# Attention in a graph network on one core: the softmax's reciprocal as exp(-ln S) on ScalarE with a Newton step on VectorE, and half of its products one step later

## The chip, the core and the metric

The kernel runs on one core of a Trainium2 chip, as one launch. A core has TensorE (PE: matmuls, PEld: their weight loads), VectorE (DVE), ScalarE (ACT), GpSimd (POOL) and SyncE (SP), each with its own queue that is worked off in order; they meet only at semaphores. The metric is the device time of one execution in microseconds (us).

## The reference

Four graph layers run one after the other on 512 nodes with 512 features, each as `x = x + layer(relu(layernorm(x)))`. The first layer holds what is changed here. Its softmax runs over the heads (`axis=1` of `n h m`), not over the nodes:

```
q = (x @ Wq + bq).reshape(N, H, HEAD)      # N = 512, H = 8, HEAD = 64
k = (x @ Wk + bk).reshape(N, H, HEAD)
v = (x @ Wv + bv).reshape(N, H, HEAD)
scores = jnp.einsum('nhd,mhd->nhm', q, k) / np.sqrt(HEAD)
scores = jnp.where(adj[:, None, :] == 0, -1000000000.0, scores)
attn = jax.nn.softmax(scores, axis=1)
attn_out = jnp.einsum('nhm,mhd->nhd', attn, v).reshape(N, D_OUT)
h1 = _layer_norm(x + attn_out @ Wo + bo, g1, be1)
ff = jax.nn.relu(h1 @ W1 + b1) @ W2 + b2
return _layer_norm(h1 + ff, g2, be2)
```

After it come a mean over edges with two products, four experts of two layers with a gate, and a last layer with normalised degrees.

## The kernel before

Everything stays in the core's memory. Float32 matrices are split into a high and a low part, and a product of two takes three matmuls. The weights, 27 matrices of 1 MB, come in through two staging buffers; ScalarE makes the high part and GpSimd the low part. In the first 95 us the kernel also counts the edges into a 512 x 512 matrix.

Attention is worked off in STEPS = 8 steps. Step i handles 128 of the m nodes (`i % 4`) against 256 of the n nodes (`i // 4`), for all 8 heads: a tile of 128 partitions x 8 heads x 256 columns. The heads go in two groups of four, g = 0 and 1. For each step:

- TensorE, `scores(i, g)` (L1212, L1216): masks with `no_edge` and multiplies k by q into the accumulator banks.
- ScalarE, `coarse_scores(i, g)` (L573): copies a group's scores to bf16.
- VectorE, `maxima(i)` (L814, L816, L819): the maximum over the heads, `m_bf`.
- TensorE, `centre(i, g)` (L1223): subtracts the maximum from the scores.
- ScalarE, `exponentials(i)` (L559): two Exp, one for each group, 128 x 1024 each, into one of three buffers `e_sb`.
- VectorE: the sum S over the heads in three additions (L836 to L838), its reciprocal (L839), and `probabilities` twice (L352), which multiplies four heads at a time by 1/S.
- TensorE, `values(i, part_no)` (L1238): multiplies the probabilities by v, two steps later, a group at a time.

Each queue is written out by hand, in this order. VectorE's loop body i begins with `maxima(i + 1)`, then sums, reciprocal and products of step i; body 5 has `attended_lo(0)` (L824) in between. ScalarE's body i is `exponentials(i)`, `coarse_scores(i + 1, 1)`, in body 5 `attended_hi(0)`, then `coarse_scores(i + 2, 0)`. TensorE's body i is `centre(i, 0)`, `centre(i, 1)`, `values(i - 2, 0)`, `scores(i + 1, 1)`, `values(i - 2, 1)`, `scores(i + 2, 0)`. Behind the last step VectorE goes on with the first layer norm (`h1_start(0)`, L850). Activation functions of the kernel before are Copy, Identity, Relu, Abs and Exp; it never asks for Ln.

Of the kernel before, what the change touches and what calls it, by code (L numbers as in the profile page):

```python
# [26 lines left out]
ACT = mybir.ActivationFunctionType  # L27
F32 = mybir.dt.float32
# [6 lines left out]
P = 128  # L35
# [4 lines left out]
def build(nc, d, out):  # L40
# [6 lines left out]
    HEADS = 8  # L47
# [4 lines left out]
    HN = N // 2  # L52
    STEPS = 2 * NT
# [14 lines left out]
    def region(size):  # L68
        start = at[0]
        at[0] += size  # L70
        return start

    def place(name, shape, dt, offset):
        return nc.alloc_sbuf_tensor_at(name, shape, dt, offset=offset)

    MAT = NT * D * 4
    rW, rX, rH, rT, rCT, rQK, rVZ, rEP, rM = (region(k * MAT) for k in (6, 1, 1, 2, 2, 4, 4, 3, 1))
# [13 lines left out]
    k_sb = place("k_sb", [P, PAIRS, N], F32, rQK + MAT)  # L91
    v_sb = place("v_sb", [P, NT, D], F32, rQK + 2 * MAT)
    half_sum = place("half_sum", [P, HEADS // 2, HN], F32, rQK + 3 * MAT)
    ff_hi = place("ff_hi", [P, FT, N], F32R, rQK)
    ff_lo = place("ff_lo", [P, FT, N], F32R, rQK + 2 * MAT)
    R_hi = place("R_hi", [P, NT, D], F32R, rQK)
# [40 lines left out]
    rsum = place("rsum", [P, 2, HN], F32, rS)  # L137
# [94 lines left out]
    with ctx:  # L232
        ps = ctx.enter_context(nc.psum_tensor("ps", [P, 8, 512], F32))

        def sem(name):
            return ctx.enter_context(nc.semaphore(name))
# [26 lines left out]
        rinv_made = sem("rinv_made")  # L263
# [16 lines left out]
        coarse_made, max_read = sem("coarse_made"), sem("max_read")  # L280
        score_done, max_done, centred = sem("score_done"), sem("max_done"), sem("centred")
        exp_done, prob_done = sem("exp_done"), sem("prob_done")
        pv_done = sem("pv_done")
        att_hi_made, att_lo_made = sem("att_hi_made"), sem("att_lo_made")
        bo_added, b2_added, be2_added, bias1_added = sem("bo_added"), sem("b2_added"), sem("be2_added"), sem("bias1_added")
# [51 lines left out]
        def group_scores(i, g):  # L337
            bank = slot_bank(i, g)
            return ps[:, bank:bank + 2, :].rearrange("p b (w n) -> p w b n", w=2)
# [5 lines left out]
        def attended():  # L345

            return ps[:, 0:2, :].rearrange("p b (w n) -> p (b w) n", w=2)

        def probabilities(engine, i, heads):

            e = e_bufs[i % E_BUFS][:, heads]
            return engine.tensor_tensor(e, e, rsum[:, i % 2:i % 2 + 1, :].to_broadcast(list(e.shape)), ALU.mult)  # L352
# [61 lines left out]
        def _(gp):  # L414
# [31 lines left out]
            def add_row(i, t, target, done):  # L446
                slot = rows_in[i][1]
                if t == 0:
                    gp.wait_ge(row_in[slot], 16 * (1 + sum(s == slot for _, s in rows_in[:i])))
                ins = gp.tensor_tensor(target[:, t, :], target[:, t, :], row[slot][:], ALU.add)  # L450
                ins.then_inc(done, 1)
# [37 lines left out]
        def _(act):  # L489
# [63 lines left out]
            def exponentials(i):  # L553
                for g in range(2):
                    if i >= E_BUFS:
                        act.wait_ge(pv_done, 2 * (i - E_BUFS) + g + 1)
                    act.wait_ge(centred, 2 * i + g + 1)
                    heads = e_bufs[i % E_BUFS][:, g * HEADS // 2:(g + 1) * HEADS // 2]
                    nc.scalar.activation(heads.rearrange("p (w b) n -> p w b n", w=2), group_scores(i, g), ACT.Exp,  # L559
                                         scale=SCALE).then_inc(exp_done, 1)  # L560

            def attended_hi(half):
                act.wait_ge(pv_done, 2 * NT * (half + 1))
                nc.scalar.activation(T_hi[:, :, half * HN:(half + 1) * HN], attended(), ACT.Copy)\
                  .then_inc(att_hi_made, 1)

            def coarse_scores(i, g):

                act.wait_ge(score_done, 2 * i + g + 1)
                if i >= 1:  # L570
                    act.wait_ge(max_read, i)
                heads = s_bf[:, g * HEADS // 2:(g + 1) * HEADS // 2]
                nc.scalar.activation(heads.rearrange("p (w b) n -> p w b n", w=2), group_scores(i, g), ACT.Copy)\  # L573
                  .then_inc(coarse_made, 1)
# [3 lines left out]
            coarse_scores(1, 0)  # L578
            for i in range(STEPS):
                exponentials(i)  # L580
                if i + 1 < STEPS:
                    coarse_scores(i + 1, 1)
                if i == NT + 1:
                    attended_hi(0)
                if i + 2 < STEPS:
                    coarse_scores(i + 2, 0)
            attended_hi(1)
            for t in range(NT // 2):
                transposed_hi(T1, None, t)
# [68 lines left out]
        def _(v):  # L658
            order = [0]

            def link(ins):

                order[0] += 1
                ins.then_inc(dve, 1)
                v.wait_ge(dve, order[0])
# [24 lines left out]
            def wait_row(i):  # L690
                slot = rows_in[i][1]
                v.wait_ge(row_in[slot], 16 * (1 + sum(s == slot for _, s in rows_in[:i])))
                return row[slot]
# [116 lines left out]
            def maxima(i):  # L810
                v.wait_ge(coarse_made, 2 * (i + 1))
                if i >= 1:
                    v.wait_ge(max_done, i)
                nc.vector.tensor_tensor(s_max[:], s_bf[:, 0:4], s_bf[:, 4:8], ALU.max).then_inc(max_read, 1)  # L814
                v.wait_ge(max_read, i + 1)
                link(nc.vector.tensor_tensor(s_max[:, 0:2], s_max[:, 0:2], s_max[:, 2:4], ALU.max))  # L816
                if i >= 1:
                    v.wait_ge(centred, 2 * i)
                nc.vector.tensor_tensor(m_bf[:], s_max[:, 0], s_max[:, 1], ALU.max).then_inc(max_done, 1)  # L819

            def attended_lo(half):
                cols = slice(half * HN, (half + 1) * HN)
                v.wait_ge(att_hi_made, half + 1)
                nc.vector.tensor_tensor(T_lo[:, :, cols], attended(), f32(T_hi[:, :, cols]),  # L824
                                        ALU.subtract).then_inc(att_lo_made, 1)

            maxima(0)
            for i in range(STEPS):
                e = e_bufs[i % E_BUFS]
                if i + 1 < STEPS:  # L830
                    maxima(i + 1)
                if i == NT + 1:
                    attended_lo(0)
                v.wait_ge(exp_done, 2 * (i + 1))
                r = rsum[:, i % 2, :]
                link(nc.vector.tensor_tensor(half_sum[:], e[:, 0:4], e[:, 4:8], ALU.add))  # L836
                link(nc.vector.tensor_tensor(half_sum[:, 0:2], half_sum[:, 0:2], half_sum[:, 2:4], ALU.add))
                link(nc.vector.tensor_tensor(r, half_sum[:, 0], half_sum[:, 1], ALU.add))  # L838
                nc.vector.reciprocal(r, r).then_inc(rinv_made, 1)  # L839
                v.wait_ge(rinv_made, i + 1)  # L840
                probabilities(nc.vector, i, slice(0, HEADS // 2)).then_inc(prob_done, 1)
                probabilities(nc.vector, i, slice(HEADS // 2, HEADS)).then_inc(prob_done, 1)

            g1_row, be1_row = wait_row(GAMMA1), wait_row(BETA1)
# [606 lines left out]
```

## Time and profile before

| | |
|---|---|
| median of 3 runs | 541.41 us (540.43 to 541.88) |
| profiled execution | 541.99 us, of which the span of the trace is 540.2 us |
| TensorE | busy 88% of the span |
| VectorE | busy 62% |
| ScalarE | busy 40% |
| attention steps, first `maxima` to the first layer norm | 107.26 to 177.24 us |

A timeline row is: start in us, duration in us, engine, line, operation, tiles, count, and in brackets the idle time before it with what released it. PE stands for matmuls, DVE for VectorE, ACT for ScalarE. Rows of merged instructions give their common duration.

### The profile page before, as it was taken

How to read it: one execution, taken by the hardware profiler on the slowest of the kernel's cores; microseconds unless marked ns; L12 is line 12 of the kernel's file. 1: busy time of each engine (PE TensorE's matmuls, PEld its weight loads, DVE VectorE, ACT ScalarE, POOL GpSimd, SP SyncE). 2: the span in 40 equal slices, each digit the busy share in tenths (PEclk: the TensorE clock that was granted, in tenths of full speed). 3: DMA queues.
4: the chain of work that ended last, by engine and by line, in shares of the span. 5: the costliest groups of instructions: out<-in, count | busy, mean ns of one | idle time of the engine just before them, and what ended most of it. 6: DMA issues, size and time to landing. Idle time of an engine off the chain costs nothing.

```text
span 540.2 us, 6721 instructions
## 1 busy us (share of the span) xinstructions
PE 477.6 (88%) x2299; PEld 368.7 (68%) x2299; DVE 336.2 (62%) x625; ACT 213.6 (40%) x268; POOL 172.6 (32%) x105
## 2 busy tenths in 40 slices
PE   3769889669787689996999999999999999999894
PEld 2657667323344579885777888888888888888683
DVE  5998695668999779849448623263334435233756
ACT  5994792355451315213415123403431342124222
POOL 3930300300000159742835033333441454153100
PEclk9997999897998798997998799999999999999999
DMA  8711100020000003340221004322222222220002
GB/s 261 199 39 58 66 13 0 30 89 0 1 0 2 0 14 103 99 164 12 97 79 49 31 2 136 96 79 73 103 78 79 78 98 78 79 78 1 0 1 78
DMA packets 22474, 34.34 MB, mean 64 GB/s; under 512 B 5680, under 2 KB 5936, under 8 KB 22448
## 3 DMA queue, kind: packets, MB, share of 16 engines
q1 hardware_dynamic: 22448, 33.98, 18.7%
q8 instruction: 18, 0.29, 0.2%
q14 instruction: 8, 0.07, 0.0%
HBM read 32.93 MB, written 1.05 MB: 63 GB/s over the span
## 4 chain that ended last, share of the span: by engine, by line
PE 64%; DVE 22%; issue 7%; ACT 3%; DVEq 2%; DMA 1%; SPq 0%; POOL 0%
PE ps L1079 17%; PE ps L1080 17%; PE ps L1081 17%; PE ps L1137 3%; PE ps L1107 2%; PE ps L1108 2%; DVE rsum L839 2%; DVE e_sb L352 2%; DVE stats L670 2%; DVE one_src L735 2%; DVE half_sum L836 1%; DMA w_stage<-in_L_gnn_Wq 1%; PE ps L1092 1%; PE ps L1216 1%; DVE h_sb L685 1%
## 5 line engine op out<-in xcount | busy, mean ns | idle before, releaser
L431 POOL TENSOR_TENSOR w_lo<-w_stage,w_hi 128x1024 fp32r<-128x1024 f32 x27 | 66.1, 2447 | 208.0 <-ACT w_hi L494 208.0
L494 ACT ACTIVATE w_hi<-w_stage 128x2048 fp32r<-128x2048 f32 x27 | 51.5, 1909 | 76.9 <-PE ps L1081 75.2
L435 POOL TENSOR_TENSOR w_lo<-w_stage,w_hi 128x1024 fp32r<-128x1024 f32 x26 | 66.4, 2553 | 0.0
L1079 PE MATMUL ps<-T_hi,w_hi 128*128 128x512 f32 (+1 forms) x144 | 56.1, 390 | 7.1 <-DVE T_lo L699 7.1
L444 POOL TENSOR_TENSOR rstd<-vareps,scalars 128x1 f32<-128x1 f32 x24 | 15.8, 657 | 133.9 <-DVE vareps L672 133.9
L1080 PE MATMUL ps<-T_lo,w_hi 128*128 128x512 f32 (+1 forms) x144 | 55.5, 385 | 0.0
L1081 PE MATMUL ps<-T_hi,w_lo 128*128 128x512 f32 (+1 forms) x144 | 55.2, 383 | 0.0
L1079 PE MATMUL ps<-w_hi,hid_hi 128*128 128x512 f32 x128 | 49.8, 389 | 0.0
L1080 PE MATMUL ps<-w_lo,hid_hi 128*128 128x512 f32 x128 | 49.8, 389 | 0.0
L1081 PE MATMUL ps<-w_hi,hid_lo 128*128 128x512 f32 x128 | 49.8, 389 | 0.0
L735 DVE TENSOR_SCALAR one_src<-iota_n,edge_m,edge_w 128x256 f16 x128 | 46.3, 403 | 0.0
L1012 DVE TENSOR_SCALAR tmp<-ps,bl 128x512 f32<-128x512 f32 x16 | 12.0, 751 | 53.5 <-ACT hid_hi L632 53.5
L1137 PE MATMUL ps<-one_src,one_dst 128*128 x256 | 34.8, 285 | 8.3 <-DVE one_src L735 6.8
L1079 PEld LDWEIGHTS ps<-T_hi,w_hi 128*128 128x128 f32 x144 | 29.4, 204 | 12.8 <-DVE T_lo L699 8.0
L1137 PEld LDWEIGHTS ps<-one_src,one_dst 128*128 x256 | 25.2, 99 | 17.8 <-issue 10.5
L1079 PE MATMUL ps<-w_hi,T_hi 128*128 128x512 f32 x80 | 34.6, 433 | 0.5 <-DVE T_lo L699 0.4
L1080 PE MATMUL ps<-w_lo,T_hi 128*128 128x512 f32 x80 | 33.1, 414 | 0.0
L1081 PE MATMUL ps<-w_hi,T_lo 128*128 128x512 f32 x80 | 32.7, 409 | 0.0
L1092 PE MATMUL ps<-ident,h_sb 128*128 128x128 f32 x80 | 15.5, 332 | 19.4 <-ACT h_sb L499 14.6
L1081 PEld LDWEIGHTS ps<-T_hi,w_lo 128*128 128x128 f32 x144 | 29.2, 203 | 4.9
L1080 PEld LDWEIGHTS ps<-T_lo,w_hi 128*128 128x128 f32 x144 | 29.3, 203 | 4.7
L733 DVE TENSOR_SCALAR one_dst<-iota_n,edge_m 128x256 f16 x64 | 26.3, 411 | 6.6 <-PE ps L1137 6.6
(175 smaller groups left out, 1011.1 us busy)
## 6 DMA issues: line engine op xcount, KB each, us to landing
w_stage<-in_L_gnn_Wr SPq DMA_DIRECT2D x8, 1024.0 KB, 5.2
w_stage<-in_L_gnn_Wl SPq DMA_DIRECT2D x8, 1024.0 KB, 5.3
w_stage<-in_L_gnn_W SPq DMA_DIRECT2D x5, 1024.0 KB, 5.3
x_sb<-in_x SPq DMA_DIRECT2D x4, 256.0 KB, 3.1
w_stage<-in_L_gnn_Wq SPq DMA_DIRECT2D x1, 1024.0 KB, 7.4
w_stage<-in_L_gnn_Wk SPq DMA_DIRECT2D x1, 1024.0 KB, 10.2
w_stage<-in_L_gnn_Wv SPq DMA_DIRECT2D x1, 1024.0 KB, 7.5
w_stage<-in_L_gnn_Wo SPq DMA_DIRECT2D x1, 1024.0 KB, 7.4
```

The lines of the kernel that those rows point to most:

```text
L431: first = gp.tensor_tensor(w_lo[s][:, 0:2], stage[s][:, 0:2], f32(w_hi[s][:, 0:2]), ALU.subtract)
L435: gp.tensor_tensor(w_lo[s][:, 2:4], stage[s][:, 2:4], f32(w_hi[s][:, 2:4]), ALU.subtract)\
L444: gp.tensor_tensor(rstd[:, n - 1:n], vareps[:, n - 1:n], half_neg, ALU.pow).then_inc(ln_rstd, 1)
L494: nc.scalar.activation(w_hi[u % 2][:], stage[u % 2][:], ACT.Copy).then_inc(hi_made, 1)
L733: nc.vector.tensor_scalar(one_dst[:, bass.ds(slot, 1), :].squeeze(1), iota_n[:, 0:HALF], edge_m[:, 1, bass.ds(c, 1)], None, ALU.is_equal)
L735: last = nc.vector.tensor_scalar(one_src[:, bass.ds(slot, 1), :].squeeze(1), iota_n[:, 0:HALF], edge_m[:, 0, bass.ds(c, 1)], edge_w[:, bas ...
L1012: link(nc.vector.tensor_scalar(tmp[:, j, :], ps[:, j, :], bl0[:, e, j:j + 1], 0.0, ALU.add, ALU.max))
L1079: nc.tensor.matmul(goal, a_hi, b_hi, start=start, stop=False, **kw)
L1080: nc.tensor.matmul(goal, a_hi, b_lo, start=False, stop=False, **kw)
L1081: return nc.tensor.matmul(goal, a_lo, b_hi, start=False, stop=stop, **kw)
L1092: last = nc.tensor.transpose(ps[:, bank, col(j)], h_sb[:, t, col(j)], ident[:])
L1137: last = nc.tensor.matmul(ps[:, 7, m * HALF:(m + 1) * HALF], cols, rows, start=False, stop=False, skip_group_check=True)
```

## The change

The division moves. VectorE now makes -S (with `scalar_tensor_tensor`, into `rsum`) and signals `sums_made`. ScalarE takes the logarithm of S into `log_sum`, waits for that, and puts exp(-ln S) into `guess`. VectorE then makes one Newton step: `residue` = -S times guess, and r = (residue + 2) times guess. Between the sums and the wait for the guess, VectorE multiplies the second four heads of the step before, which so far followed the first four at once. On ScalarE the two new activations of step i stand in body i + 1, behind `exponentials(i + 1)`; those of the last step stand behind the loop, and the last second half of the products stands behind VectorE's loop.

```
+            def reciprocal_guess(i):
+                act.wait_ge(sums_made, i + 1)
+                nc.scalar.activation(log_sum[:], rsum[:, i % 2, :], ACT.Ln, scale=-1.0).then_inc(log_made, 1)
+                act.wait_ge(log_made, i + 1)
+                nc.scalar.activation(guess[:], log_sum[:], ACT.Exp, scale=-1.0).then_inc(guess_made, 1)
+
             coarse_scores(1, 0)
             for i in range(STEPS):
                 exponentials(i)
+                if i >= 1:
+                    reciprocal_guess(i - 1)
                 if i + 1 < STEPS:
                     coarse_scores(i + 1, 1)
                 if i == NT + 1:
                     attended_hi(0)
                 if i + 2 < STEPS:
                     coarse_scores(i + 2, 0)
+            reciprocal_guess(STEPS - 1)
             attended_hi(1)
...
                 r = rsum[:, i % 2, :]
                 link(nc.vector.tensor_tensor(half_sum[:], e[:, 0:4], e[:, 4:8], ALU.add))
                 link(nc.vector.tensor_tensor(half_sum[:, 0:2], half_sum[:, 0:2], half_sum[:, 2:4], ALU.add))
-                link(nc.vector.tensor_tensor(r, half_sum[:, 0], half_sum[:, 1], ALU.add))
-                nc.vector.reciprocal(r, r).then_inc(rinv_made, 1)
+                nc.vector.scalar_tensor_tensor(r, half_sum[:, 0], -1.0, half_sum[:, 1], ALU.mult, ALU.subtract)\
+                  .then_inc(sums_made, 1)
+                if i >= 1:
+                    probabilities(nc.vector, i - 1, slice(HEADS // 2, HEADS)).then_inc(prob_done, 1)
+                v.wait_ge(sums_made, i + 1)
+                v.wait_ge(guess_made, i + 1)
+                link(nc.vector.tensor_tensor(residue[:], r, guess[:], ALU.mult))
+                nc.vector.scalar_tensor_tensor(r, residue[:], 2.0, guess[:], ALU.add, ALU.mult).then_inc(rinv_made, 1)
                 v.wait_ge(rinv_made, i + 1)
                 probabilities(nc.vector, i, slice(0, HEADS // 2)).then_inc(prob_done, 1)
-                probabilities(nc.vector, i, slice(HEADS // 2, HEADS)).then_inc(prob_done, 1)
+            probabilities(nc.vector, STEPS - 1, slice(HEADS // 2, HEADS)).then_inc(prob_done, 1)
```

The new tiles `log_sum`, `guess` and `residue` (128 x 256 float32 each) lie in free memory behind `half_sum`, and there are three new semaphores.

## Rows read from the trace of the kernel before

**Rows 1.** The page: busy shares of the span, and the chain by engine.

```profile
PE 477.6 (88%) x2299; PEld 368.7 (68%) x2299; DVE 336.2 (62%) x625; ACT 213.6 (40%) x268; POOL 172.6 (32%) x105
...
PE 64%; DVE 22%; issue 7%; ACT 3%; DVEq 2%; DMA 1%; SPq 0%; POOL 0%
```

**Rows 2.** Busy time by stretch: length, PE, PEld, DVE, ACT, POOL, then TensorE's clock.

```profile
121.19:130.16 8.97, 7.44 (x31) 3.01 (x32) 7.77 (x10) 3.99 (x4) 0.00 (x0) 0.62 0.00 0
...
138.06:145.94 7.88, 6.27 (x40) 2.88 (x40) 7.67 (x10) 3.98 (x4) 0.00 (x0) 1.00 0.01 2
...
153.83:162.85 9.02, 7.40 (x42) 4.25 (x42) 8.81 (x11) 3.98 (x4) 0.00 (x0) 1.00 0.00 0
```

**Rows 3.** Timeline of VectorE: steps 1 and 4, and the end.

```profile
113.29 0.69 DVE L814 TENSOR_TENSOR s_max<-s_bf 128x1024 bf16<-128x1024 bf16 x1 [4.55 <-ACT s_bf L573]
...
138.06 0.68 DVE L814 TENSOR_TENSOR s_max<-s_bf 128x1024 bf16<-128x1024 bf16 x1
138.78 0.42 DVE L816 TENSOR_TENSOR s_max<-s_max 128x512 bf16<-128x512 bf16 x1
139.23 0.29 DVE L819 TENSOR_TENSOR m_bf<-s_max 128x256 bf16<-128x256 bf16 x1
139.44 1.22 DVE L836 TENSOR_TENSOR half_sum<-e_sb 128x1024 f32<-128x1024 f32 x1
140.69 0.69 DVE L837 TENSOR_TENSOR half_sum<-half_sum 128x512 f32<-128x512 f32 x1
141.42 0.42 DVE L838 TENSOR_TENSOR rsum<-half_sum 128x256 f32<-128x256 f32 x1
141.88 1.75 DVE L839 RECIPROCAL rsum<-rsum 128x256 f32<-128x256 f32 x1
143.67 2.36 DVE L352 TENSOR_TENSOR e_sb<-e_sb,rsum 128x1024 f32<-128x1024 f32 x2
145.94 0.68 DVE L814 TENSOR_TENSOR s_max<-s_bf 128x1024 bf16<-128x1024 bf16 x1
...
162.85 0.68 DVE L814 TENSOR_TENSOR s_max<-s_bf 128x1024 bf16<-128x1024 bf16 x1
...
177.24 0.68 DVE L850 TENSOR_TENSOR h_sb<-ps,h_sb 128x512 f32<-128x512 f32 x1
...
182.96 0.75 DVE L688 SCALAR_TENSOR_TENSOR h_sb<-h_sb,rstd,row 128x512 f32<-128x512 f32 x1
```

**Rows 4.** Timeline of TensorE in the same step.

```profile
139.58 1.04 PE L1223 MATMUL ps<-m_bf,neg_ident 128*128 128x512 bf16 x4 [1.58 <-DVE m_bf L819]
...
144.72 1.13 PE L1216 MATMUL ps<-q_sb,k_sb 64*128 64x256 f32 x8
```

**Rows 5.** Timeline of ScalarE in the same step.

```profile
140.28 1.94 ACT L559 ACTIVATE e_sb<-ps 128x1024 f32<-128x1024 f32 x2 [0.43 <-PE ps L1223]
143.28 1.02 ACT L573 ACTIVATE s_bf<-ps 128x1024 bf16<-128x1024 f32 x1 [1.06 <-PE ps L1216]
146.72 1.02 ACT L573 ACTIVATE s_bf<-ps 128x1024 bf16<-128x1024 f32 x1 [2.42 <-DVE s_max L814]
```

**Rows 6.** Timeline of ScalarE near the start of the kernel.

```profile
0.74 1.28 ACT L499 ACT_TABLE_LOAD   x1 [0.74 <-PEq L1442]
5.53 0.81 ACT L499 ACTIVATE h_sb<-x_sb,shift,rstd 128x512 f32<-128x512 f32 x1 [3.51 <-DVE shift L679]
...
16.62 1.69 ACT L523 ACTIVATE distance<-iota_n,edge_neg 128x256 f16<-128x256 f16 x4
18.44 1.15 ACT L528 ACTIVATE one_dst<-distance,scalars 128x1024 f16 x1
```

**Rows 7.** ScalarE's groups by line: busy us, mean ns of one, idle before.

```profile
L650 ACT ACTIVATE R_hi<-tmp 128x512 fp32r<-128x512 f32 x4 | 2.5, 633 | 7.5 <-DVE tmp L1054 7.5
...
L626 ACT ACTIVATE gate<-logit 128x16 f32<-128x16 f32 x1 | 0.2, 216 | 1.3 <-DVE logit L989 1.3
```

**Rows 8.** Timeline of TensorE and ScalarE where step 2 begins.

```profile
118.68 1.13 PE L1216 MATMUL ps<-q_sb,k_sb 64*128 64x256 f32 x8
122.72 1.89 PE L1223 MATMUL ps<-m_bf,neg_ident 128*128 128x512 bf16 x4 [2.90 <-DVE m_bf L819]
...
123.79 1.94 ACT L559 ACTIVATE e_sb<-ps 128x1024 f32<-128x1024 f32 x2 [0.80 <-PE ps L1223]
```

More of the change, by code:

```diff
@@ L93, in build @@
     half_sum = place("half_sum", [P, HEADS // 2, HN], F32, rQK + 3 * MAT)
+    log_sum = place("log_sum", [P, HN], F32, rQK + 3 * MAT + 4 * HN * 4)
+    guess = place("guess", [P, HN], F32, rQK + 3 * MAT + 5 * HN * 4)
+    residue = place("residue", [P, HN], F32, rQK + 3 * MAT + 6 * HN * 4)
     ff_hi = place("ff_hi", [P, FT, N], F32R, rQK)
@@ L282, in build @@
         exp_done, prob_done = sem("exp_done"), sem("prob_done")
+        sums_made, log_made, guess_made = sem("sums_made"), sem("log_made"), sem("guess_made")
         pv_done = sem("pv_done")
```

## The prediction, made before the changed kernel ran

> **What bounds the kernel now.** I read the page first: TensorE is busy 88% of the span and holds 64% of the chain, VectorE 22% of it [rows 1]. An average hides the stage, so I cut the attention steps into stretches. In a settled step of 7.88 us VectorE is busy 7.67, TensorE 6.27 and ScalarE 3.98 [rows 2]. Here VectorE is the bound, and TensorE is not. The timeline of VectorE shows why: its eight instructions of a step follow each other with gaps of 0.02 to 0.04 us, and the next step's L814 starts as the last product ends [rows 3]. In start-to-start times the period is 1.38 (maxima) + 2.44 (three additions) + 1.79 (reciprocal) + 2.27 (two products) = 7.88 us.
>
> ScalarE has slack, but its queue lies inside the same loop: L819 starts at 139.23, `centre` at 139.58, the Exp pair at 140.28 for 1.94 us, to 142.22 [rows 3 to 5]. Before, this loop closes with room, since the sums of step i need only the Exp of step i, which are a period old. From 113.29 (L814 of `maxima(1)`) to 162.85 (`maxima(7)`) six periods pass, 49.56 us; from there to the layer norm at 177.24 another 14.39 us [rows 3]. Behind 177.24 the next stage starts on VectorE, so what the last product is late, the rest of the kernel is late.
>
> **What the change does to VectorE's work.** Removed: the reciprocal, 1.79. Added: a TENSOR_TENSOR of 256 columns, as L838, 0.46, and a SCALAR_TENSOR_TENSOR of 256 columns. The trace has that one at 512 columns only, 0.75; the step from 512 to 256 is 0.27 for L837 against L838, so 0.48 (bounds 0.46 to 0.75) [rows 3]. The third addition becomes such an instruction too, +0.02 at least. Net: -0.83 us a step if the guess is never waited for, a period of 7.05. This is the gain on offer, some 6.6 us over 8 steps. The delayed product costs nothing in itself; it covers 1.14 us of the wait.
>
> **What it adds to ScalarE.** An activation of 256 columns lies between L626 (16 columns, 0.216) and L650 (512, 0.633) [rows 7]; on the line between them 0.42 us each, bounds 0.22 and 0.63. The second waits for the first; in the nearest pair of that kind L528 starts 0.13 after the end of L523 [rows 6].
>
> The item without a direct row is the table. The trace has ACT_TABLE_LOAD as an instruction of ScalarE's queue, 1.28 us, once, in front of the first Relu; what it loaded served Relu, Copy, Abs, Identity and every Exp after it [rows 6]. Ln is in no instruction of before. Either the loaded table has Ln (no further load), or one load brings a table with both (one load), or Ln and Exp come from different tables, and then every step has two: one between the Exp pair and Ln, one between Ln and the guess. No row decides between 0 and 16 loads. I take 16: the only choice in the trace was made for a Relu alone, before any Exp was due, so I read the choice as made for the one function at hand, and for Ln alone nothing favours a table that also has Exp. Both ends stay below.
>
> On this the Trainium skill speaks. "ScalarE: Activation LUTs", section "Table sets: the hidden batching unit", lists Exp's usual set without Ln, and a set with both, and says that Ln followed by Exp is one load; by that the sum would be the rival with a gain below. The same page, section "What ACT_TABLE_LOAD costs", gives 1283 ns for the load, as the trace has it, but about 2.66 us for a whole switch; that is the second rival.
>
> **The sum with two loads a step.** `reciprocal_guess(i - 1)` is queued behind `exponentials(i)`. VectorE's `maxima(i + 1)` stands behind the products that wait for this guess, and `exponentials(i + 1)` waits for these maxima. So a new loop goes round every step, where before VectorE only worked off its list. From L814 of `maxima(i)`:
>
> to `centre` 1.52, to the Exp pair 0.70, the pair 1.94 [rows 3 to 5]; load 1.28, Ln 0.42, gap 0.13, load 1.28, Exp 0.42 [rows 6, 7]; to VectorE 0.05; Newton 0.46 + 0.48; first product 1.14 [rows 3]; then L814 of `maxima(i + 1)`. Sum 9.82 us.
>
> VectorE's own work (7.05) fits, waiting some 2.8 us a step. `coarse_scores(i + 1, 1)`, queued behind the guess, runs at 7.7 to 8.7, before 9.82: hidden. `attended_lo(0)` of body 5, which made that period 9.02 [rows 2], falls into the wait: hidden too. If it had no cover it would cost 1.14.
>
> The clock is the next term. Behind 119.81 TensorE was idle for 2.90 us, `centre` then took 1.89 instead of 1.04, the clock was 0.62 on average in that stretch (full speed is 1.00, the half of it is 1.2 GHz), and the Exp pair came 1.07 behind `centre` instead of 0.70 [rows 2, 4, 8]. In a 9.82 period TensorE idles from 7.8 to 11.3, 3.5 us, so it should fall again. But a slow step ends TensorE's work about 2.7 us later (the step from 121.19 did), which shortens the next idle time to some 1.2 us. I take every second of the six periods, 3 x 0.37 = 1.1 us; bounds none and all, 0 and 2.2.
>
> Six periods: 6 x 9.82 + 1.1 = 60.0, against 49.56: +10.5. The last part: 9.82, then three additions 2.44, then the last guess. Its first load needs no data and can run ahead of the wait, as the one at 0.74 did, 4.8 us ahead of its activation [rows 6]. So 0.10 + 0.42 + 0.13 + 1.28 + 0.42 + 0.05 = 2.40, then Newton 0.94, two products 2.27: 17.87 against 14.39, +3.5. Together +14.0 us. The profiled execution was 541.99 with a span of 540.2; it would come to 556.0. It stood 0.6 over the median of 541.41, so for the median I say 555.4.
>
> **Bounds of this case.** Activations at 0.22 or 0.63: -3 or +3 (15 of them in the loop). Clock: -1.1 or +1.1. A bubble of 0.1 to 0.2 behind a load: up to +3. The load of the last guess not ahead: +1.3. Overlap at the loads: -1.5. Combined, 549 to 566.
>
> **Rivals.**
> *One table serves both (other side of zero).* Mechanism: one more load at most, in step 0, 1.28. A guess is then ready at 4.16 + 0.42 + 0.13 + 0.42 + 0.05 = 5.18 behind L814, and L814 comes again at 5.18 + 0.94 + 1.14 = 7.26. Five periods of it, and one of 1.38 + 1.14 + 2.44 + 1.14 + 0.94 + 1.14 = 8.2 with `attended_lo`, are 44.5 against 49.56, -5.1; last part 7.26 + 2.44 + 1.14 + 0.94 + 2.27 = 14.05, -0.3; load +1.3. Together -4.1: 537.3 us (534 to 540). It speaks for it that a single load served five functions [rows 6]; against it, nothing but my reading of the choice. It is decided by the price between Exp pair and guess: the change gains only while loads and activations there stay below some 1.6 us, and two loads alone are 2.56. Chance 0.13.
> *A switch costs more than its row.* At 0.74 the load's end was followed by 3.51 us of a wait for VectorE, which could hide 1.38 us of settling [rows 6]. With 2.66 in place of 1.28 the six periods grow by 2.76 each and the end by some 4.1: +21 more, 576 us. Chance 0.06.
> *It comes out even.* Loads only where they run in a wait, or a lower clock that eats the gain of the first rival: 540 to 543. Chance 0.03.
> *The forecast.* Two loads a step at the row's price: 0.78.
>
> **Numbers.** About 0.3% (1.6 us) is what a measurement of this kernel tells from no change. Faster by more than that 0.12, within it 0.04, slower 0.84. The forecast's own range, 549 to 566, leaves out 0.22 with the other cases, so I draw it out a little, to 548 and 569, where a switch costs part of what the second rival says.
>
> **What would show it.** In the changed profile: 16 more ACT_TABLE_LOAD, two in each step, of 1.28 us; L839's line gone; VectorE's busy time near 7.05 in a period of 9.8 to 10.2, its idle time ended by ScalarE's guess; `coarse_scores` of group 1 directly behind the guess; TensorE's clock below 1.00 in several steps; the stages behind attention as before, only later. Wrong: one load more or none, VectorE without a wait at the Newton step, and a period near 7.3; or gaps of over 1 us behind each load, and a period near 12.6. The step most likely to fail is the count of loads.

## The result, and the profile after

The changed kernel takes 553.91 us in the median (551.38 to 554.12) against 541.64 for the kernel before, measured beside it: ratio 1.0216, 95% interval 1.0186 to 1.0246, slower. The forecast was 555.4, range 548 to 569.

The profiled execution took 554.12 us with a span of 552.3, 12.1 us more than before. ScalarE's groups by line (busy us, mean ns of one, idle time before) show the loads:

```profile
L568 ACT ACT_TABLE_LOAD x8 | 10.3, 1283 | 0.1
L570 ACT ACT_TABLE_LOAD x8 | 10.3, 1283 | 0.1
...
L568 ACT ACTIVATE log_sum<-rsum 128x256 f32<-128x256 f32 x8 | 3.3, 417 | 3.4 <-DVE rsum L851 3.3
L570 ACT ACTIVATE guess<-log_sum 128x256 f32<-128x256 f32 x8 | 3.3, 417 | 0.1
```

Sixteen loads, two a step, 20.5 us in all, beside the one at the start that the kernel before has too [rows 6]. VectorE's timeline of the step that begins at 143.14, and the starts of the others:

```profile
113.47 0.69 DVE L827 TENSOR_TENSOR s_max<-s_bf 128x1024 bf16<-128x1024 bf16 x1 [4.55 <-ACT s_bf L583]
...
143.14 0.68 DVE L827 TENSOR_TENSOR s_max<-s_bf 128x1024 bf16<-128x1024 bf16 x1
143.86 0.42 DVE L829 TENSOR_TENSOR s_max<-s_max 128x512 bf16<-128x512 bf16 x1
144.32 0.29 DVE L832 TENSOR_TENSOR m_bf<-s_max 128x256 bf16<-128x256 bf16 x1
144.53 1.22 DVE L849 TENSOR_TENSOR half_sum<-e_sb 128x1024 f32<-128x1024 f32 x1
145.78 0.69 DVE L850 TENSOR_TENSOR half_sum<-half_sum 128x512 f32<-128x512 f32 x1
146.51 0.43 DVE L851 SCALAR_TENSOR_TENSOR rsum<-half_sum 128x256 f32<-128x256 f32 x1
146.85 1.22 DVE L356 TENSOR_TENSOR e_sb<-e_sb,rsum 128x1024 f32<-128x1024 f32 x1
151.30 0.42 DVE L857 TENSOR_TENSOR residue<-rsum,guess 128x256 f32<-128x256 f32 x1 [3.23 <-ACT guess L570]
151.76 0.42 DVE L858 SCALAR_TENSOR_TENSOR rsum<-residue,guess 128x256 f32<-128x256 f32 x1
152.22 1.22 DVE L356 TENSOR_TENSOR e_sb<-e_sb,rsum 128x1024 f32<-128x1024 f32 x1
153.36 0.68 DVE L827 TENSOR_TENSOR s_max<-s_bf 128x1024 bf16<-128x1024 bf16 x1
...
173.79 0.68 DVE L827 TENSOR_TENSOR s_max<-s_bf 128x1024 bf16<-128x1024 bf16 x1
...
191.46 0.69 DVE L869 TENSOR_TENSOR h_sb<-ps,h_sb 128x512 f32<-128x512 f32 x1
...
203.22 0.69 DVE L869 TENSOR_TENSOR h_sb<-ps,h_sb 128x512 f32<-128x512 f32 x1 [2.75 <-PE ps L1100]
```

It answers to [rows 3]. VectorE, which had no gap, waits 3.23 us in front of the Newton step, for ScalarE's guess. The six periods from 113.47 to 173.79 are 60.3 us (49.56 before), the last part from 173.79 to 191.46 is 17.7 (14.39). ScalarE in the same step:

```profile
143.92 1.02 ACT L583 ACTIVATE s_bf<-ps 128x1024 bf16<-128x1024 f32 x1 [2.03 <-DVE s_max L827]
145.80 1.94 ACT L563 ACTIVATE e_sb<-ps 128x1024 f32<-128x1024 f32 x2 [0.86 <-PE ps L1242]
147.76 1.28 ACT L568 ACT_TABLE_LOAD   x1
149.05 0.42 ACT L568 ACTIVATE log_sum<-rsum 128x256 f32<-128x256 f32 x1
149.49 1.28 ACT L570 ACT_TABLE_LOAD   x1
150.78 0.42 ACT L570 ACTIVATE guess<-log_sum 128x256 f32<-128x256 f32 x1
151.10 1.00 ACT L583 ACTIVATE s_bf<-ps 128x1024 bf16<-128x1024 f32 x1
```

The chain of the forecast stands there in its order: Exp pair, load, Ln, load, guess, without an idle moment, and the coarse copy behind them. The activation behind a load starts 0.01 us after the load's end (147.76 + 1.28 = 149.04).

From the first maxima to the layer norm attention takes 84.02 us (107.44 to 191.46) against 69.98, +14.04. Only 12.1 us of it arrive at the end. The rest comes back in the stage behind: from the layer norm's first tile to its third, which waits for TensorE, it is 11.76 us, and 13.90 before (177.24 to 191.14). I call this stretch the transition. Behind it the two profiles take the same time, 349.1 us to the end of the span.

### The profile page after: what moved, and what is told of

It reads as the page before. It is cut to its first block, busy times and chain, and to the rows that moved or that the text cites. A ratio compares the mean times of both kernels' runs of the same rounds, so it can differ in the third digit from the quotient of the medians.

```text
span 552.3 us, 6769 instructions
## 1 busy us (share of the span) xinstructions
PE 481.4 (87%) x2299; PEld 368.4 (67%) x2299; DVE 328.9 (60%) x633; ACT 240.1 (43%) x300; POOL 172.6 (31%) x105
## 4 chain that ended last, share of the span: by engine, by line
PE 63%; DVE 17%; issue 8%; ACT 8%; DVEq 2%; DMA 1%; SPq 0%; POOL 0%; ACTq 0%
PE ps L1098 17%; PE ps L1099 16%; PE ps L1100 16%; PE ps L1156 3%; PE ps L1126 2%; ACT e_sb L563 2%; PE ps L1127 2%; DVE one_src L748 2%; ACT L568 2%; DVE stats L683 2%; DMA w_stage<-in_L_gnn_Wq 1%; PE ps L1242 1%; DVE s_max L827 1%; DVE h_sb L698 1%; PE ps L1111 1%
## 5 line engine op out<-in xcount | busy, mean ns | idle before, releaser
L748 DVE TENSOR_SCALAR one_src<-iota_n,edge_m,edge_w 128x256 f16 x128 | 48.7, 425 | 0.0
L1044 DVE TENSOR_TENSOR part<-ps,row_bl 128x512 f32<-128x512 f32 x16 | 11.1, 692 | 29.9 <-PE ps L1100 29.9
```

The source lines that it names most:

```text
L748: last = nc.vector.tensor_scalar(one_src[:, bass.ds(slot, 1), :].squeeze(1), iota_n[:, 0:HALF], edge_m[:, 0, bass.ds(c, 1)], edge_w[:, bas ...
L1044: nc.vector.tensor_tensor(part[:, t, :], ps[:, t, :], row_bl[e % 2][:], ALU.add)\
```

## The experiments

Attention, transition and what lies behind it, up to the end of the span, are read from the one profiled execution of each kernel. The median is over its timed runs. The ratios further down are to runs of the kernel before made beside those of the experiment; these have medians from 541.72 to 542.34 us. All columns are in us.

| kernel | attention | transition | behind | profiled | median |
|---|---|---|---|---|---|
| before | 69.98 | 13.90 | 349.1 | 541.99 | 541.41 |
| changed | 84.02 | 11.76 | 349.1 | 554.12 | 553.91 |
| one_table | 64.70 | 14.90 | 350.8 | 540.08 | 536.74 |
| one_table_undelayed | 71.93 | 13.07 | 350.8 | 544.90 | 544.74 |
| delay_alone | 68.89 | 12.26 | 350.8 | 540.55 | 542.23 |
| wo_late | 68.90 | 13.76 | 350.8 | 542.75 | 542.77 |
| four_loads | 105.51 | 13.70 | 351.2 | 578.30 | 578.74 |
| copy_guess | 80.72 | 13.15 | 350.8 | 553.28 | 552.19 |
| before_warm | 70.03 | 11.54 | 350.8 | 541.12 | 540.59 |
| one_table_warm | 64.68 | 12.98 | 351.0 | 538.33 | 538.20 |
| copy_guess_early | 76.59 | 12.55 | 351.1 | 549.92 | 549.26 |
| one_table_again | 64.64 | 12.38 | 349.0 | 534.25 | 537.51 |
| one_table_filled | 64.66 | 11.54 | 350.4 | 534.96 | 536.38 |

The column "behind" matters for what follows. No edit touches the stages behind the transition, and yet they take 349.0 to 349.1 us in three profiles and 350.4 to 351.2 in the other ten, one_table and its repetition one_table_again among them on different sides. So differences of up to 2 us in a profiled time can come from there. In the attention steps too, the kernel before has one step lengthened by a half clock (8.97 us instead of 7.88), which delay_alone and wo_late do not have: their attention is 1.1 us shorter for that.

**One table for both functions.** The loss should vanish if the loads are all of it.

```
             for t in range(NT):
+            nc.scalar.add_instruction(mybir.InstLoadActFuncSet(name=..., act_func_set_id=6))
                 normalise(LN0, t, h_sb, x_sb, ACT.Relu)
```

Theory (the loads in the loop are the whole loss): one load in the trace, period from L814's successor to the next 7.26 us instead of about 10.1, attention some 5 us shorter than before, and the 2.1 us that the changed kernel won back between attention and the next layer norm stay: 535 to 537 us. Rival (the hand-over to ScalarE and back, not the loads, makes the loop long): period stays over 8.5 us and the time above 544 us.

Measured: ratio to before 0.9891 (0.9871 to 0.9912), 536.74 us. A second set of runs with the same edit, one_table_again, gave 0.9917 (0.989 to 0.9944). One load of 1.28 us remains, at the start of the kernel. Of one_table_again, first ScalarE's timeline, then VectorE's, the same step in both:

```profile
136.85 1.94 ACT L564 ACTIVATE e_sb<-ps 128x1024 f32<-128x1024 f32 x2 [0.43 <-PE ps L1243]
138.67 0.42 ACT L569 ACTIVATE log_sum<-rsum 128x256 f32<-128x256 f32 x1
139.12 0.42 ACT L571 ACTIVATE guess<-log_sum 128x256 f32<-128x256 f32 x1
```

```profile
134.62 0.68 DVE L828 TENSOR_TENSOR s_max<-s_bf 128x1024 bf16<-128x1024 bf16 x1
...
138.33 1.22 DVE L356 TENSOR_TENSOR e_sb<-e_sb,rsum 128x1024 f32<-128x1024 f32 x1
139.64 0.43 DVE L858 TENSOR_TENSOR residue<-rsum,guess 128x256 f32<-128x256 f32 x1
...
141.70 0.69 DVE L828 TENSOR_TENSOR s_max<-s_bf 128x1024 bf16<-128x1024 bf16 x1
```

The guess is ready at 139.54, and VectorE's product ends at 139.55, so almost nothing of the wait is left. The settled period is 7.08 us, against 7.05 of VectorE's own work, the forecast's floor. There is nothing to spare: `residue` starts 0.10 us behind the end of the guess, as it does in the changed kernel, where VectorE waits for it (151.20 to 151.30). The loop through ScalarE and VectorE's own work have become about equally long. So the hand-over to ScalarE (the rival) is not what costs; the loads turned a gain of some 5 us into a loss of 12. Of the theory the transition did not hold: in one_table's profile it is 14.90, not some 12, and 12.38 in that of one_table_again.

**Without the delay.** The same, with both halves of the products together again.

```
-                if i >= 1:
-                    probabilities(nc.vector, i - 1, slice(HEADS // 2, HEADS)).then_inc(prob_done, 1)
                 v.wait_ge(sums_made, i + 1)
...
                 probabilities(nc.vector, i, slice(0, HEADS // 2)).then_inc(prob_done, 1)
+                probabilities(nc.vector, i, slice(HEADS // 2, HEADS)).then_inc(prob_done, 1)
```

> As one_table, but the second half of the products follows the first at once. Theory: the delayed product covers the wait for the guess (ready 5.18 us into the period, sums ready at 3.82), so without it the period is 5.18 + 0.94 + 2.27 = 8.39 us, longer than the 7.88 of before: 542 to 544 us, and the transition's 2.1 us are not won. Rival (delaying has no worth of its own): equal to one_table within 1 us.

Measured: 544.74 us, ratio 1.0043 (1.0027 to 1.006). VectorE's timeline:

```profile
138.88 0.68 DVE L828 TENSOR_TENSOR s_max<-s_bf 128x1024 bf16<-128x1024 bf16 x1
...
143.90 0.43 DVE L856 TENSOR_TENSOR residue<-rsum,guess 128x256 f32<-128x256 f32 x1 [1.23 <-ACT guess L571]
...
147.09 0.69 DVE L828 TENSOR_TENSOR s_max<-s_bf 128x1024 bf16<-128x1024 bf16 x1
```

The period is 8.21 (8.39 expected), the wait of 1.23 lies open. The time of 544.74 is 0.7 above the range. So the delay is worth some 8 us beside one_table, and without it even one table makes the kernel slower than before. The change needs both of its halves, and the table.

**The delay alone.** The reciprocal stays on VectorE.

```
+                if i >= 1:
+                    probabilities(nc.vector, i - 1, slice(HEADS // 2, HEADS)).then_inc(prob_done, 1)
                 nc.vector.reciprocal(r, r).then_inc(rinv_made, 1)
                 v.wait_ge(rinv_made, i + 1)
                 probabilities(nc.vector, i, slice(0, HEADS // 2)).then_inc(prob_done, 1)
-                probabilities(nc.vector, i, slice(HEADS // 2, HEADS)).then_inc(prob_done, 1)
+            probabilities(nc.vector, STEPS - 1, slice(HEADS // 2, HEADS)).then_inc(prob_done, 1)
```

> The reciprocal stays on VectorE, only the second half of the products comes one step later. Theory: attention as long as before (VectorE has the same work, period 7.88), but TensorE gets its last but one product later, so that the second tile of the output projection stands next to the layer norm and keeps the clock up: 2.1 us faster, 539.3 us. Rival (the 2.1 us have to do with something else in the changed kernel): 541.4 us, no change.

Measured: ratio 0.9995 (0.998 to 1.0009), no change. The settled period is 7.89, as expected. The 2.1 us did not come, and the result is that of the rival. The profile does have a transition of 12.26, 1.6 us shorter than that of before, but the stretch behind it is 1.7 us longer. The median over twelve runs stays, and they spread from 540.43 to 543.67.

**The output projection's second tile later.**

```
+            pe.wait_ge(rinv_made, STEPS)
             rows_tile(wo_bank(1), 1, w, wo_done)
```

> The kernel before, with the second tile of the output projection held back on TensorE until the last reciprocal, 1.8 us later. Theory (filler work next to the idle stretch keeps the clock up): granted clock near 1.00 behind attention, 1.5 to 2.1 us faster, 539.5 us. Rival (order does not matter there): the same or up to 1 us slower, 541.4 to 542.4 us.

Measured: ratio 1.0003 (0.9991 to 1.0016). No change, again the rival. It does not test the theory well: the wait it adds put 3.0 us of idle time in front of the tile (TensorE's waits, longest first), so idle time was only moved. The clock did not stay up either (0.65 from 184 to 186, 0.50 from 186 to 188), and the layer norm's third tile came as late as before:

```profile
PE ps L1079 <- DVE rsum L839: 3.0, 1, 3.0
```

**Two more loads in each step.**

```
+                for table in (0, 5, 0):
+                    nc.scalar.add_instruction(mybir.InstLoadActFuncSet(name=..., act_func_set_id=table))
                 nc.scalar.activation(guess[:], log_sum[:], ACT.Exp, scale=-1.0).then_inc(guess_made, 1)
```

> Two more table loads between Ln and the guess in every step, nothing else. Theory (each load between Exp pair and guess costs its row, 1.28 us, and nothing behind it): period 2.56 us longer in all six, both last parts 2.56 longer too, 8 x 2.56 = 20.5 us over the changed kernel: 573 to 576 us. Rival (loads back to back are cheaper, or each brings a settling time of its own): under 565 or over 585 us.

Measured: 578.74 us, ratio 1.069 (1.067 to 1.071), 24.8 over the changed kernel and 2.7 above my range. ScalarE's timeline:

```profile
130.31 0.42 ACT L568 ACTIVATE log_sum<-rsum 128x256 f32<-128x256 f32 x1
130.74 3.86 ACT L571 ACT_TABLE_LOAD   x3
134.61 0.42 ACT L573 ACTIVATE guess<-log_sum 128x256 f32<-128x256 f32 x1
```

Three loads take 3.86, 1.29 each, with nothing behind them: two more than the one of the changed kernel. Attention grows by 21.5 us. Five of the six periods are 2.57 to 2.59 longer than the same ones of the changed kernel, so 16 more loads are 20.6; the other 0.9 are two further steps in which `centre` ran at half clock, 0.4 each (1.89 us at 138.72 and 189.90; 1.04 in the changed kernel at 134.88 and 175.31). The rest of the 24.2 us between the two profiles is 1.9 in the transition (13.70 against 11.76), 2.1 behind it and 1.3 less ahead of attention. A load's price is its row's.

**The guess as a Copy.** One of the two loads moves. The products are then no longer divided by S.

```
-                nc.scalar.activation(guess[:], log_sum[:], ACT.Exp, scale=-1.0).then_inc(guess_made, 1)
+                nc.scalar.activation(guess[:], log_sum[:], ACT.Copy, scale=-1.0).then_inc(guess_made, 1)
```

 Theory (a load costs what it holds up where it stands): the coarse copy of ScalarE ends 1.80 us into the period, the load then ends at 3.08, 0.4 to 0.9 us after the scores are centred, so the period falls from 10.0 by some 0.4 us, and the end by 1.3 to 1.7: about 549 to 551 us. Rival 1 (the load hides wholly in ScalarE's idle time there): 544 us. Rival 2 (only the number of loads counts, which is almost the same): 553 us.

Measured: 552.19 us, ratio 1.0187 (1.0169 to 1.0204); the theory's 549 to 551 missed, between it and rival 2. ScalarE's timeline:

```profile
141.31 1.02 ACT L583 ACTIVATE s_bf<-ps 128x1024 bf16<-128x1024 f32 x1 [2.03 <-DVE s_max L827]
143.18 1.28 ACT L563 ACT_TABLE_LOAD   x1 [0.84 <-PE ps L1242]
144.47 1.94 ACT L563 ACTIVATE e_sb<-ps 128x1024 f32<-128x1024 f32 x2
```

ScalarE was free at 142.33, but the load started at 143.18, when the scores were centred: it stood behind the waits of the Exp pair, and its whole 1.28 us lay on the loop again, period 10.21. I had counted on what [rows 6] show, a load that runs ahead of the wait. There the activation has one wait; the Exp pair has two from step 3 on. In step 2 of this same kernel, where it still has one, the load starts at 123.17, directly behind a coarse copy. That fits, but no run changes only the number of waits. The kernel has 13 loads in the attention steps instead of 16, and its 3.3 us of attention are won where a load is gone (the first period, 8.45 instead of 9.74, and the last part, 16.43 instead of 17.67) and in the second period (9.40 instead of 10.15). The settled ones gained nothing.

**The same load, written out ahead of the waits.**

```
                 if i + 2 < STEPS:
                     coarse_scores(i + 2, 0)
+                if 1 <= i < STEPS - 1:
+                    nc.scalar.add_instruction(mybir.InstLoadActFuncSet(name=..., act_func_set_id=0))
```

> As copy_guess (its output is not the reference's either), but the load of Exp's table is written out directly behind the coarse copies, ahead of the two waits of the Exp pair. Theory (in copy_guess the load stood behind both waits and so never used ScalarE's idle time; only its place decides): it now runs from 1.8 to 3.1 us into the period instead of from 2.6 to 3.9, so the Exp pair starts 0.8 us earlier in each step from 3 on, period 9.4 instead of 10.2: 4 us under copy_guess, 548 us. Rival (the number of loads in the loop decides): 552 us as before.

Measured: 549.26 us, ratio 1.013 (1.0104 to 1.0156), 2.9 under copy_guess (4 expected); attention 4.1 shorter. ScalarE's timeline:

```profile
141.90 1.02 ACT L583 ACTIVATE s_bf<-ps 128x1024 bf16<-128x1024 f32 x1 [2.03 <-DVE s_max L830]
142.94 1.28 ACT L600 ACT_TABLE_LOAD   x1
144.24 1.94 ACT L563 ACTIVATE e_sb<-ps 128x1024 f32<-128x1024 f32 x2
```

The load follows the coarse copy at once, the period is 9.39 (9.4 expected), from the second on all alike. The number of loads in the loop is that of copy_guess, 13. So it is the place of a load that decides what it costs: part of this one is now in idle time.

**Filler for the clock.** Two tests of the transition, with matmuls of no use while TensorE waits for the layer norm.

```
             values(STEPS - 1, 1)
+            for _ in range(14):
+                nc.tensor.matmul(ps[:, 4, :], neg_ident[:], twice(m_bf[:]), start=True, stop=True)
             for t in range(NT // 2):
```

> The kernel before with 14 matmuls of no use on TensorE (into a bank that the next product overwrites) in the 3.4 us in which it waits for the first layer norm. Theory (the half clock that follows that idle time lengthens the products behind it): granted clock 1.00 from there to the third layer norm tile, 1.5 to 2.1 us faster, 540 us. Rival (the end of the second tile does not hang on that clock): the same, 542 us.

> one_table with the same 14 matmuls. Theory: as before_warm, 1 to 2 us under one_table: 534.5 to 536 us, the fastest of all. Rival: the same as one_table, 536.7 us, or slower, since the matmuls themselves hold up the transposes.

Measured: before_warm 0.9967 (0.9943 to 0.999), one_table_warm 0.9935 (0.9922 to 0.9947). On the kernel before the filler shortened the transition to 11.54 us in the profile (and 1.7 us of the 2.4 were lost again behind it), and the ratio says 0.3% faster, 1.8 us; the interval allows 0.5 to 3.1, and the two medians differ by 1.1, with runs from 537.31 to 542.19. The 1.5 to 2.1 us of the theory lie inside, but the size of the gain is not settled. On one_table it gained nothing: 0.9935 is worse than the ratio of one_table, clear of its interval, and its interval overlaps that of one_table_again. TensorE had less to wait there (0.61 us in front of the transposes in one_table, 3.41 before), and the filler ran into the transposes, as its timeline shows:

```profile
177.76 3.19 PE L1298 MATMUL ps<-m_bf,neg_ident 128*128 128x512 bf16 x14
180.79 1.04 PE L1112 MATMUL ps<-ident,h_sb 128*128 128x128 f32 x8
```

In one_table the transposes began 6.92 us behind the layer norm's start (172.59 to 179.51), here 8.26 (172.53 to 180.79).

**Less filler, in two places.** Eight matmuls ahead of `values(6, 1)` (shown), four ahead of the transposes, and one_table again beside it.

```
             values(STEPS - 2, 0)
+            for _ in range(8):
+                nc.tensor.matmul(ps[:, 7, :], neg_ident[:], twice(m_bf[:]), start=True, stop=True)
             values(STEPS - 2, 1)
```

> The same as one_table, to stand beside one_table_filled on one chip. 535.5 to 537.5 us, executions apart by up to 4 us as TensorE's clock falls or not behind the attention steps.

> one_table with 8 matmuls of no use in TensorE's wait for the last but one product and 4 in its wait for the layer norm, fewer than the 14 that ended 1.3 us too late. Theory (clock): no half clock between 167 and 190 us, the first layer norm's tiles on time, 535 us in every execution and at most 1 us under one_table_again in the median. Rival (the filler costs what the clock gives): the same as one_table_again or above it.

Measured: 0.9917 (0.989 to 0.9944) and 0.9903 (0.9874 to 0.9932). The filled version has the shortest transition (11.54, as before_warm), and in its profile the granted clock is 1.00 from 160 to 206 us, as the theory has it. But its runs still spread from 534.12 to 538.48, so the promise of 535 in every execution failed, and the intervals overlap: the two can't be told apart. Both beat the kernel before by about 1%.

## Why the prediction was right

Its steps one by one, forecast against profile:

| term | forecast | measured |
|---|---|---|
| table loads | 16, of 1.28 us | 16, of 1.283 us |
| idle time behind a load | 0 | 0.01 to 0.02 |
| Ln and Exp of 256 columns | 0.42 each | 0.417 each |
| from Ln's end to the second load | 0.13 | 0.02 |
| from the guess to VectorE | 0.05 | 0.10 |
| period at full clock | 9.82 | 9.74 and 9.78 |
| period with `centre` at half clock | 10.19 | 10.15 to 10.22 |
| slow periods of six | 3 | 4 |
| six periods | 60.0 | 60.3 |
| last part | 17.87 | 17.67 |
| attention | +14.0 | +14.04 |
| stages behind attention | 0 | -2.1 |
| median | 555.4 | 553.91 |

That attention agrees to 0.1 us is luck in part: the gap behind Ln is shorter than reckoned, the last part 0.2 us shorter, and one more step at half clock makes up for them. Without the 2.1 us won behind attention the median would have been some 556 us, an estimate from 553.91 + 2.1.

**The loads.** The count was the open choice, and I had called it the step most likely to fail. It held, and four kernels bear out the price: none of the loads in the loop (one_table, -19.3 us in attention against the changed kernel), one of the two moved to two other places, and two more a step. The rival with one table was worked out at 537.3 us; one_table measured 536.74, its attention of 64.70 is 5.3 us under that of before, against 5.4 worked out. The order of the loop is right on both sides of the choice, but the closeness of these numbers is again luck in part. The 537.3 hold 1.3 us for a load in step 0 that one_table does not have. Its settled periods are 7.08, not 7.26, since Ln starts 0.12 us before the Exp pair's row ends and the gap behind Ln is 0.02; two other periods are longer for it (7.87, in which VectorE waits 0.77 us for a coarse copy, and 7.33), and the six come to 44.4 against 44.5. Shown is what one_table does. The reading behind the count, that a table is chosen for the one function at hand, was not tested by itself: the traces show that two tables were taken where one serves both, and why the program is built so was not traced.

The Trainium skill, "ScalarE: Activation LUTs", section "Table sets: the hidden batching unit", says that Ln followed by Exp is one load. The trace of the changed kernel disagrees, with two for each pair; one_table agrees that such a table exists and serves every function of this kernel. The 2.66 us for a switch in the section "What ACT_TABLE_LOAD costs" (the second rival, 576 us) do not show: 1.28 us, and the activation 0.01 to 0.02 behind.

**The clock.** Of four periods in which `centre` took 1.89 instead of 1.04 us the forecast had three. TensorE's timeline shows that the alternation I had reasoned stopped after two turns:

```profile
144.67 1.89 PE L1242 MATMUL ps<-m_bf,neg_ident 128*128 128x512 bf16 x4 [3.52 <-DVE m_bf L832]
...
154.88 1.89 PE L1242 MATMUL ps<-m_bf,neg_ident 128*128 128x512 bf16 x4 [2.62 <-DVE m_bf L832]
...
165.10 1.89 PE L1242 MATMUL ps<-m_bf,neg_ident 128*128 128x512 bf16 x4 [2.61 <-DVE m_bf L832]
```

In the step at 124.73 the clock stayed at half until about 130.4, and only 1.24 us of idle time remained in front of the next `centre`, at 134.88, which ran at full clock. In the steps at 144.67 and 154.88 the clock was back at full after some 2.8 us. TensorE was done earlier, 2.6 us of idle time remained, and the clock fell again each time. Behind the step at 165.10 the output projection's first tile fills that time (171.04 to 174.06), and the last `centre` ran at full clock. The same idle time does not always bring the same clock: in copy_guess_early `centre` took 1.04 us at 142.65 and at 152.04 and 1.89 at 161.43, each time behind 2.44 us of idle time.

**What the sum left out.** "What the last product is late, the rest of the kernel is late" was wrong by 2.1 us, the transition. The granted clock (after PE's, PEld's and the other engines' busy times) of the changed kernel, from 183 to 195:

```profile
183.00:187.00 4.00, 1.97 (x8) 0.77 (x8) 3.93 (x5) 0.97 (x2) 0.00 (x0) 0.50 0.00 0
...
189.00:191.00 2.00, 2.00 (x7) 1.55 (x6) 1.97 (x3) 0.00 (x0) 0.00 (x0) 0.50 0.00 0
191.00:193.00 2.00, 2.00 (x9) 1.59 (x8) 1.93 (x4) 0.00 (x0) 0.00 (x0) 0.78 0.00 0
193.00:195.00 2.00, 2.00 (x18) 1.53 (x18) 1.75 (x5) 0.00 (x0) 0.55 (x1) 1.00 0.00 0
```

And of the kernel before, around its layer norm at 177.24:

```profile
179.00:181.00 2.00, 0.00 (x0) 0.00 (x0) 1.90 (x6) 0.98 (x1) 0.65 (x2) 1.00 0.00 0
...
185.00:187.00 2.00, 2.00 (x9) 2.00 (x10) 1.13 (x2) 2.00 (x5) 0.00 (x0) 0.50 0.00 0
187.00:189.00 2.00, 2.00 (x6) 1.52 (x6) 0.00 (x0) 0.51 (x1) 0.00 (x0) 0.50 0.00 0
189.00:191.00 2.00, 2.00 (x9) 1.59 (x8) 0.00 (x0) 0.00 (x0) 0.00 (x0) 0.77 0.00 0
```

Before, the half clock (1.2 GHz) falls on the products of the next stage, for which VectorE then waits; in the changed kernel the later product and the second projection tile behind it took the half clock, and it was over soon after the layer norm began (191.46). That fits both profiles, and before_warm, where filler brought the transition to 11.54. But delay_alone, which moves the same product and tile, did not get faster in the median. Where the clock falls differs between executions of one kernel: one_table's profiled run took 540.08 us with a transition of 14.90, that of the same kernel in one_table_again 534.25 with 12.38. So it stays open whether the 2.1 us are typical of the changed kernel or of the execution that was profiled; only one_table has a second trace, and the medians can't separate 2 us of transition from the rest.

## What to carry to other kernels

Before moving work to ScalarE, ask which activation tables the functions lie in: here a pair of Ln and Exp brought two loads of 1.28 us into every step, inside the loop that bound the kernel, and one explicit load of a table with both made the same change 1% faster than the old kernel instead of 2% slower. Moved work pays where its latency is covered, so price the whole round trip against the work left to do meanwhile (here a delayed product of 1.1 us covered a wait of 1.2 us in every step, 8 us in all). What a load costs here is decided by its place: written out ahead of a wait it was hidden in part (copy_guess_early, period 9.39), behind the wait it was paid in full (copy_guess, 10.21). And a gain of 2 us in one profile of this kernel is no result, since a stretch that no edit touched differs by as much between profiles.

## What the runs showed of the hardware that I had not expected

- A table load ran ahead of the wait of an activation with one wait (at 0.74 in [rows 6]; at 181.43 in the changed kernel, 4.6 us ahead of its Ln), but behind the waits of one with two (copy_guess, 143.18, from step 3 on). That the number of waits is the reason is not shown.
- An activation that follows another directly starts before the first one's row ends: in one_table_again Ln starts at 138.67, the Exp pair ends at 138.79. Behind a load there is no such overlap.
- The time of one kernel spreads by up to 1% between executions (534.25 to 539.49 us for one_table_again). The two profiles of that kernel, one_table and one_table_again, are 5.8 us apart: 1.5 before attention, 2.5 in the transition (granted clock 0.50 from 182 to 184 in the first, 1.00 in the second) and 1.8 behind it, where the half clock ahead of the first expert lasted about 10 us in the first and 7 in the second.
